# A graph layer with residual and norm on one core: both halves of a dense pair through TensorE in one go

## The chip, the cores and the metric

The kernel runs on one core of one Trainium2 chip. The metric is the device time of one execution in microseconds (us); smaller is better.

## The reference

The input is `x` (100000 nodes of 96 features, float32), 25000 edges `src -> dst` sorted by `dst`, and 32 edge features. Two convolutions with a leaky ReLU (slope 0.01) follow each other, then a residual and a norm over each row. `X` below is `x`, with all 100000 nodes in both convolutions; everything is float32.

```python
def _egnn_conv(x, src, dst, edge_attr, W_msg, W_edge, W_root, b):
    msg = x[src] @ W_msg + edge_attr @ W_edge
    agg = jax.ops.segment_max(msg, dst, num_segments=x.shape[0])
    agg = jnp.where(jnp.isneginf(agg), 0.0, agg)
    return agg + x @ W_root + b
c1 = leaky_relu(_egnn_conv(X, src, dst, edge_attr, W1_msg, W1_edge, W1_root, b1))
c2 = leaky_relu(_egnn_conv(c1, src, dst, edge_attr, W2_msg, W2_edge, W2_root, b2))
out = _layernorm(X + c2)
```

## The kernel before

A node without an incoming edge needs no aggregate: its output is `leaky(leaky(x @ W1_root + b1) @ W2_root + b2) + x`, normed. The kernel computes this for all 100000 nodes (the **dense** work), and apart from it, along the list of edges, the rows of the nodes that have incoming edges (the **edge** work), which it writes over the dense rows at the end.

**Dense work.** 98 pairs of 1024 nodes. A pair has two halves `h` of 512 nodes. Layer 1 is one matmul per half into half `h` of `ps_1` (`layer1`, L448, 96x512). ScalarE writes 0.01 times it into `c1t` (`dense_t1`, L579), VectorE takes the larger of the two (`dense_c1`, L774). Layer 2 is four matmuls per half (`layer2`, L458, 128x96 each, `c1t` as the weights) into half `h` of `ps_z`. Then ScalarE writes 0.99 times the positive part to `yo` (`dense_r`, L588), VectorE adds 0.01 times the sum and `x` (`dense_u`, L766) and both (`dense_y`, L781), takes the statistics (L792), and the two engines norm the eight rows of 96 (L605 and L802). SyncE loads `xtb` and `xn` two pairs ahead and stores `yo` (`load_pair`, `store_pair`). `ps_1` and `ps_z` exist once, with two halves each; `c1t` exists twice.

**Step d** of the dense work puts layer 2 of pair d-1 and layer 1 of pair d side by side. Each engine has its own fixed order within a step: TensorE `layer2(d-1, h)`, `layer1(d, h)` for one half, then for the other; ScalarE std(d-2), r(d-1, 0), t1(d, 0), then r(d-1, 1), t1(d, 1), norm(d-2); VectorE reciprocal and shift of d-2, u(d-1, 0), c1(d, 0), y(d-1, 0), then u, c1, y of half 1, then statistics of d-1 and its part of the norm of d-2.

**Edge work.** 49 chunks of 512 edges. Stage A (first layer): GpSimd gathers `x[src]` (four indirect DMAs per chunk, L261, a ring `g_src` of six chunks), TensorE turns them (`forward`, L434), multiplies (`product`, L438) and turns the running maxima back (L472); VectorE scans (L739). Then GpSimd scatters the maxima to a table (L283), which ScalarE's DMAs clear ahead of it. Stage B (second layer): GpSimd gathers from the table (L261), and rows of `x` by destination (L272, a ring `g_dst` of ten chunks); TensorE does `forward(g_src)`, `sums_back` of the chunk before (L505, L506, into `ps_n`), `forward(g_dst)`, a product (L438) and the root term (L542, L544); VectorE and ScalarE join these (L884, L844, L739, L904, L860; L571, L695, L657, L672). At the end GpSimd scatters the edge rows over the dense rows in `out` (L283), chunk by chunk, each chunk when the pairs below its last destination are stored (`s_stored`) and its own rows are done (`e_done`).

**How the dense steps are spread.** 14 steps run within stage A (one every 3 or 4 chunks), 35 while GpSimd scatters to the table (stage S, nothing else on TensorE), 25 within stage B (one every second chunk), and steps 75 to 98 after it, while GpSimd scatters to `out` (here: the tail). In A and B TensorE puts half 0 behind `forward(g_src)` and half 1 further down the chunk.

Of the kernel before, what the change touches and what calls it, by code (L numbers as in the profile page):

```python
# [5 lines left out]
N, D = 100000, 96  # L6
# [6 lines left out]
J = 8  # L13
HJ = J // 2
# [6 lines left out]
XR = 4  # L21
# [25 lines left out]
STEPS_A = spread(NA, NCH, 0)  # L47
STEPS_S = spread(NS, NCH, NA)
STEPS_B = spread(NM, NCH, NA + NS)
# [9 lines left out]
def gnn_kernel(nc, x, xt, src, dst, dst_next, dst_row, dst_prev, aside, eat,  # L59
# [18 lines left out]
    with ctx:  # L78
# [15 lines left out]
        wr1 = sb("wr1", [D + 1, D])  # L94
# [110 lines left out]
        d_1 = sem("d_1")  # L205
# [15 lines left out]
        def cols(j):  # L221
            return slice(j * P, (j + 1) * P)

        def row(j):
            return slice(j * D, (j + 1) * D)
# [4 lines left out]
        def half(h):  # L230
            return slice(h * CH, (h + 1) * CH)
# [90 lines left out]
        def _(sp):  # L322
# [12 lines left out]
            def load_pair(q):  # L335
                if not real(q):
                    return
                k = q % XR
                if q >= XR:
                    sp.wait_ge(d_1, 2 * (q - XR) + 2)  # L340
                sp.dma_start(xtb[0:D, k, :], xt[q]).then_inc(l_xt[k], 16)
                if q >= XR:
                    sp.wait_ge(d_y, 2 * (q - XR) + 2)
                if q < NQ - 1:
                    sp.dma_start(xn[:, k, :], x_q[q]).then_inc(l_xn[k], 16)
                else:
                    sp.dma_start(xn[0:TAIL, k, :], x_tail).then_inc(l_xn[k], 16)
# [76 lines left out]
        @block.tensor  # L424
        def _(pe):
            pe.wait_ge(s_ident, 1)
            pe.wait_ge(s_const, 9 * 16)
            pe.wait_ge(s_ones, 3)

            def forward(rows, done, landed=(), count=0):  # L430
                for r in range(TPC):
                    if landed:
                        pe.wait_ge(landed[r], count)
                    last = nc.tensor.transpose(ps_t[0:D, cols(r)], rows[:, row(r)], ident[:, :])  # L434
                last.then_inc(done, 1)

            def product(ps, w, t, done):
                nc.tensor.matmul(ps[0:D, :], w, t, start=True, stop=True).then_inc(done, 1)  # L438

            def layer1(q, h):  # L440
                if not real(q):
                    return
                k = q % XR
                if h == 0:
                    pe.wait_ge(l_xt[k], 16 * (q // XR) + 16)
                if q >= 1:
                    pe.wait_ge(d_c1, 2 * (q - 1) + h + 1)
                nc.tensor.matmul(ps_1[0:D, h, :], wr1[:, :], xtb[:, k, half(h)],  # L448
                                 start=True, stop=True).then_inc(d_1, 1)

            def layer2(q, h):
                if not real(q):
                    return
                pe.wait_ge(d_c1, 2 * q + h + 1)
                if q >= 1:
                    pe.wait_ge(d_y, 2 * (q - 1) + h + 1)
                for j in range(HJ):
                    last = nc.tensor.matmul(ps_z[:, h, row(j)], c1t[:, q % 2, cols(h * HJ + j)], wr2[:, :],  # L458
                                            start=True, stop=True)
                last.then_inc(d_2, 1)  # L460

            def dense(steps, h):
                for d in steps:
                    layer2(d - 1, h)
                    layer1(d, h)

            def maxima_back(c):
                pe.wait_ge(a_scan, c + 1)
                if c >= 1:
                    pe.wait_ge(a_nc, c)  # L470
                for r in range(TPC):
                    last = nc.tensor.transpose(ps_n[:, row(r)], mx1[:, c % 2, cols(r)], ident[0:D, 0:D])  # L472
                last.then_inc(a_n, 1)

            for t in range(NCH):
                k = t % R
                if t >= 1:
                    pe.wait_ge(a_xe, t)
                forward(g_src[:, t % RS, :], a_t, slot(l_src, t % RS), 16 * (t // RS) + 16)
                dense(STEPS_A[t], 0)  # L480
                if t >= 1:
                    maxima_back(t - 1)
                pe.wait_ge(l_ea[k], 16 * (t // R) + 16)
                if t >= 1:
                    pe.wait_ge(a_scan, t)
                pe.wait_ge(a_xe, t + 1)
                product(ps_m, wm1[:, :], xe[:, k, :], a_m)
                if t >= 1:
                    pe.wait_ge(a_rc, t)
                product(ps_r, wr1[0:D, :], xe[0:D, k, :], a_r)  # L490
                dense(STEPS_A[t], 1)
            maxima_back(NCH - 1)
            for t in range(NCH):
                for h in range(2):
                    dense(STEPS_S[t], h)

            def sums_back(c):
                pe.wait_ge(b_c1d, c + 1)
                pe.wait_ge(b_scan, c + 1)
                if c >= 1:  # L500
                    pe.wait_ge(e_y, c)
                else:
                    pe.wait_ge(a_nc, NCH)
                for r in range(TPC):
                    nc.tensor.matmul(ps_n[:, row(r)], c1d[:, c % 2, cols(r)], wr2[:, :], start=True, stop=False)  # L505
                    last = nc.tensor.matmul(ps_n[:, row(r)], mx2[:, c % 2, cols(r)], ident[0:D, 0:D],  # L506
                                            start=False, stop=True)
                last.then_inc(b_n, 1)

            for c in range(NCH + 1):  # L510
                e = NCH + c
                k = e % R
                if c < NCH:
                    if c >= 1:
                        pe.wait_ge(b_xd, c)
                    else:
                        pe.wait_ge(a_xe, NCH)
                    forward(g_src[:, e % RS, :], b_t, slot(l_src, e % RS), 16 * (e // RS) + 16)
                    dense(STEPS_B[c], 0)
                else:  # L520
                    dense(STEPS_B[c], 0)
                    dense(STEPS_B[c], 1)
                if c >= 1:
                    sums_back(c - 1)
                if c < NCH:
                    pe.wait_ge(l_dst[c % RD], 64 * (c // RD) + 64)
                    pe.wait_ge(b_z1, c + 1)
                    forward(g_dst[:, c % RD, :], b_own)
                    dense(STEPS_B[c], 1)
                    pe.wait_ge(b_c1, c + 1)  # L530
                    pe.wait_ge(l_ea[k], 16 * (e // R) + 16)
                    if c >= 1:
                        pe.wait_ge(b_scan, c)
                    else:
                        pe.wait_ge(a_scan, NCH)
                    product(ps_m, wm2[:, :], xe[:, k, :], b_m)
                    pe.wait_ge(b_xd, c + 1)
                    if c >= 1:
                        pe.wait_ge(b_c1d, c)
                    else:  # L540
                        pe.wait_ge(a_rc, NCH)
                    nc.tensor.matmul(ps_r[0:D, :], wr1[0:D, :], xd[:, c % 2, :], start=True, stop=False)  # L542
                    for r in range(TPC):
                        last = nc.tensor.matmul(ps_r[0:D, cols(r)], nat[:, c * TPC + r, :], ident[:, :],  # L544
                                                start=False, stop=r == TPC - 1)
                    last.then_inc(b_r, 1)
            for d in range(LATE + 1, NQ + 1):
                for h in range(2):
                    dense(range(d, d + 1), h)

        @block.scalar
        def _(act):
# [20 lines left out]
            def dense_t1(q, h):  # L573
                if not real(q):
                    return
                act.wait_ge(d_1, 2 * q + h + 1)
                if q >= 2:
                    act.wait_ge(d_2, 2 * (q - 2) + h + 1)
                nc.scalar.activation(c1t[0:D, q % 2, half(h)], ps_1[0:D, h, :],  # L579
                                     ACT.Copy, scale=SLOPE).then_inc(d_t1, 1)  # L580

            def dense_r(q, h):
                if not real(q):
                    return
                act.wait_ge(d_2, 2 * q + h + 1)
                if q >= YR and h == 0:
                    act.wait_ge(o_st[q % YR], 16 * (q // YR))
                nc.scalar.activation(yo[:, q % YR, halfrow(h)], ps_z[:, h, 0:HJ * D],  # L588
                                     ACT.Relu, scale=1.0 - SLOPE).then_inc(d_r, 1)
# [358 lines left out]
```

## Time and profile before

| | us |
|---|---|
| median of 3 runs (lowest, highest) | 1247.58 (1247.53, 1247.67) |
| the profiled execution's own time | 1245.89 |
| its span on the core | 1244.1 |

| engine | busy us | share of the span |
|---|---|---|
| TensorE | 1022.8 | 82% |
| GpSimd | 934.0 | 75% |
| VectorE | 822.3 | 66% |
| ScalarE | 691.9 | 56% |

The span is the stretch that the profiler saw on the core; the execution's own time has 1.8 us more around it. "Busy" counts instructions at work; GpSimd's time between two DMA issues is not in it. The mean granted clock of TensorE is 0.733 of its full speed.

### The profile page before, as it was taken

To read this page: it belongs to the slowest core of one execution; us is meant where nothing else is said; L and a number is where in the kernel's file an instruction comes from. 1 tells how busy PE (TensorE), PEld (TensorE's weight loads), DVE (VectorE), ACT (ScalarE), POOL (GpSimd) and SP (SyncE) were. 2 spreads that over 40 slices of the span, in tenths; PEclk is the share of its full clock that TensorE was granted. 3 is DMA by queue.
4 is the path that set the end of the run, shared out by engine and by line. 5 is a ranking of instruction groups with operands and counts; after the bars stand their busy time and mean duration, and the time that the engine had idled before them with its cause. 6 is when DMAs were issued, how large, how long until landed. Compare 5 with 4: busy or idle time off the path is not lost. (4 is left out here: it accounts for less than half of the span.)

```text
span 1244.1 us, 17633 instructions
## 1 busy us (share of the span) xinstructions
PE 1022.8 (82%) x4312; PEld 686.4 (55%) x4312; DVE 822.3 (66%) x1879; ACT 691.9 (56%) x1669; POOL 934.0 (75%) x986
## 2 busy tenths in 40 slices
PE   4777687789999999928888989889888899999920
PEld 2343343445666666516666666666666665666610
DVE  4454354557777777709777777777786787777730
ACT  2454354566666666606656566565565667666630
POOL 7777777777777777777777777777777777777775
PEclk9988788898555555559888888888897895555555
DMA  7877778789999777745564554655556446677520
GB/s 213 262 236 233 216 238 263 228 273 340 380 402 381 233 225 211 219 128 141 151 168 127 163 154 130 167 123 167 142 142 165 139 129 192 211 219 214 165 86 28
DMA packets 105950, 248.96 MB, mean 200 GB/s; under 512 B 26641, under 2 KB 27537, under 8 KB 105849
## 3 DMA queue, kind: packets, MB, share of 16 engines
q1 hardware_dynamic: 67432, 161.21, 42.4%
q0 software_dynamic: 31360, 48.23, 15.5%
q10 hardware_dynamic: 7056, 38.40, 8.1%
q8 instruction: 36, 0.59, 0.2%
q14 instruction: 66, 0.53, 0.1%
HBM read 141.94 MB, written 105.80 MB: 199 GB/s over the span
## 5 line engine op out<-in xcount | busy, mean ns | idle before, releaser
L458 PEld LDWEIGHTS ps_z<-wr,c1t 97*128 97x128 f32 x1568 | 305.0, 277 | 139.5 <-issue 117.2
L458 PE MATMUL ps_z<-wr,c1t 97*128 97x96 f32 x1568 | 301.0, 358 | 5.1 <-DVE yo L781 5.1
L448 PE MATMUL ps<-xtb,wr 97*96 97x512 f32 x392 | 304.0, 870 | 0.0
L605 ACT ACTIVATE yo<-yo,shift,rstd 128x96 f32<-128x96 f32 x638 | 238.1, 456 | 0.5 <-DVE shift L755 0.5
L283 POOL DMA_INDIRECT out<-nat,end_i x196 | 188.2, 960 | 59.8 <-issue 34.8
L283 POOL DMA_INDIRECT agg_table<-nat,end_i x196 | 188.0, 959 | 59.8 <-issue 48.2
L261 POOL DMA_INDIRECT g_src<-agg_table,src_i x196 | 186.2, 950 | 59.8 <-issue 55.8
L261 POOL DMA_INDIRECT g_src<-in_x,src_i x196 | 185.1, 944 | 61.0 <-issue 48.5
L272 POOL DMA_INDIRECT g_dst<-in_x,own_i x196 | 185.8, 948 | 59.7 <-issue 56.4
L774 DVE TENSOR_TENSOR c1t<-ps,c1t 96x512 f32<-96x512 f32 x196 | 134.3, 685 | 80.8 <-ACT c1t L579 80.3
L739 DVE TENSOR_TENSOR_SCAN mx<-mask,mx,ps_m 96x512 f32<-96x512 f32 x96 | 122.0, 1271 | 88.8 <-PE ps_m L438 88.7
L579 ACT ACTIVATE c1t<-ps 96x512 f32<-96x512 f32 x196 | 114.9, 586 | 88.3 <-PE ps L448 88.2
L438 PE MATMUL ps_m<-xe,wm 128*96 128x512 f32 x196 | 129.5, 748 | 31.8 <-ACT xe L571 25.2
L505 PE MATMUL ps_n<-wr,c1d 97*128 97x96 f32 x392 | 91.8, 322 | 57.7 <-DVE c1d L904 57.7
L766 DVE SCALAR_TENSOR_TENSOR ps_z<-ps_z,xn 128x384 f32<-128x384 f32 x196 | 110.6, 564 | 34.4 <-ACT yo L588 34.1
L434 PE MATMUL ps_t<-ident,g_src 128*96 128x128 f32 x392 | 71.4, 292 | 69.7 <-DMA g_src<-in_x,src_i 34.1
L588 ACT ACTIVATE yo<-ps_z 128x384 f32<-128x384 f32 x196 | 94.3, 481 | 59.7 <-PE ps_z L458 56.8
L505 PEld LDWEIGHTS ps_n<-wr,c1d 97*128 97x128 f32 x392 | 74.8, 231 | 77.3 <-DVE c1d L904 71.6
L792 DVE BATCH_NORM_STATS2 stat<-yo 128x6 f32<-128x192 f32 x392 | 112.7, 350 | 2.5
L434 PEld LDWEIGHTS ps_t<-ident,g_src 128*96 128x96 f32 x392 | 48.7, 133 | 114.5 <-issue 69.6
L781 DVE TENSOR_TENSOR yo<-ps_z,yo 128x384 f32<-128x384 f32 x196 | 106.6, 544 | 0.1
L506 PE MATMUL ps_n<-ident,mx 96*128 96x96 f32 x392 | 92.9, 327 | 0.0
(60 smaller groups left out, 1149.9 us busy)
## 6 DMA issues: line engine op xcount, KB each, us to landing
xtb<-in_xt SPq DMA_DIRECT2D x98, 384.0 KB, 5.7
xn<-in_x SPq DMA_DIRECT2D x97, 384.0 KB, 6.2
out<-yo SPq DMA_DIRECT2D x97, 384.0 KB, 5.8
agg_table<-zero ACTq DMA_DIRECT2D x48, 768.0 KB, 7.2
mask<-mask_row SPq DMA_DIRECT2D x98, 192.0 KB, 4.9
root_keep<-rt SPq DMA_DIRECT2D x49, 192.0 KB, 4.4
rt<-root_keep SPq DMA_DIRECT2D x49, 192.0 KB
xe<-in_eat SPq DMA_DIRECT2D x98, 64.0 KB, 3.4
```

The source lines that it names most:

```text
L261: nc.gpsimd.indirect_dma_start(out=g_src[:, e % RS, row(r)], out_offset=None, in_=rows, in_offset=bass.IndirectOffsetOnAxis(ap=src_i[:, t: ...
L272: nc.gpsimd.indirect_dma_start(out=g_dst[:, c % RD, row(r)], out_offset=None, in_=x, in_offset=bass.IndirectOffsetOnAxis(ap=own_i[:, t:t + ...
L283: nc.gpsimd.indirect_dma_start(out=rows, out_offset=bass.IndirectOffsetOnAxis(ap=end_i[:, t:t + 1], axis=0), in_=nat[:, t, :], in_offset=N ...
L434: last = nc.tensor.transpose(ps_t[0:D, cols(r)], rows[:, row(r)], ident[:, :])
L438: nc.tensor.matmul(ps[0:D, :], w, t, start=True, stop=True).then_inc(done, 1)
L448: nc.tensor.matmul(ps_1[0:D, h, :], wr1[:, :], xtb[:, k, half(h)], start=True, stop=True).then_inc(d_1, 1)
L458: last = nc.tensor.matmul(ps_z[:, h, row(j)], c1t[:, q % 2, cols(h * HJ + j)], wr2[:, :], start=True, stop=True)
L505: nc.tensor.matmul(ps_n[:, row(r)], c1d[:, c % 2, cols(r)], wr2[:, :], start=True, stop=False)
L579: nc.scalar.activation(c1t[0:D, q % 2, half(h)], ps_1[0:D, h, :], ACT.Copy, scale=SLOPE).then_inc(d_t1, 1)
L605: last = nc.scalar.activation(yo[:, q % YR, row(j)], yo[:, q % YR, row(j)], ACT.Identity, bias=shift[:, q % 2, j:j + 1], scale=rstd[:, q % ...
L739: V.tensor_tensor_scan(mx[:, c % 2, :], mask[:, mk, :], ps_m[0:D, :], first, ALU.min, ALU.max).then_inc(done, 1)
L774: V.tensor_tensor(t, ps_1[0:D, h, :], t, ALU.max).then_inc(d_c1, 1)
```

## The change

TensorE no longer works by halves. `layer1(q)` waits once, for both halves of `c1` of pair q-1, issues both 96x512 matmuls and raises `d_1` once, after the second. `layer2(q)` waits once, for both halves of `c1` and both halves of `y`, issues all eight matmuls and raises `d_2` once, after the eighth. Both halves stand where half 0 stood; the place of half 1 further down a chunk is gone. ScalarE, VectorE and SyncE keep their instructions and their order; the waits of ScalarE (`dense_t1`, `dense_r`) and of SyncE (`load_pair`) count pairs now, not halves. No instruction that computes is added or removed.

```diff
@@ -337,7 +337,7 @@
                     return
                 k = q % XR
                 if q >= XR:
-                    sp.wait_ge(d_1, 2 * (q - XR) + 2)
+                    sp.wait_ge(d_1, q - XR + 1)
                 sp.dma_start(xtb[0:D, k, :], xt[q]).then_inc(l_xt[k], 16)
                 if q >= XR:
                     sp.wait_ge(d_y, 2 * (q - XR) + 2)
@@ -437,32 +437,32 @@
             def product(ps, w, t, done):
                 nc.tensor.matmul(ps[0:D, :], w, t, start=True, stop=True).then_inc(done, 1)
 
-            def layer1(q, h):
+            def layer1(q):
                 if not real(q):
                     return
                 k = q % XR
-                if h == 0:
-                    pe.wait_ge(l_xt[k], 16 * (q // XR) + 16)
+                pe.wait_ge(l_xt[k], 16 * (q // XR) + 16)
                 if q >= 1:
-                    pe.wait_ge(d_c1, 2 * (q - 1) + h + 1)
-                nc.tensor.matmul(ps_1[0:D, h, :], wr1[:, :], xtb[:, k, half(h)],
-                                 start=True, stop=True).then_inc(d_1, 1)
-
-            def layer2(q, h):
-                if not real(q):
-                    return
-                pe.wait_ge(d_c1, 2 * q + h + 1)
+                    pe.wait_ge(d_c1, 2 * q)
+                for h in range(2):
+                    last = nc.tensor.matmul(ps_1[0:D, h, :], wr1[:, :], xtb[:, k, half(h)], start=True, stop=True)
+                last.then_inc(d_1, 1)
+
+            def layer2(q):
+                if not real(q):
+                    return
+                pe.wait_ge(d_c1, 2 * q + 2)
                 if q >= 1:
-                    pe.wait_ge(d_y, 2 * (q - 1) + h + 1)
-                for j in range(HJ):
-                    last = nc.tensor.matmul(ps_z[:, h, row(j)], c1t[:, q % 2, cols(h * HJ + j)], wr2[:, :],
+                    pe.wait_ge(d_y, 2 * q)
+                for j in range(J):
+                    last = nc.tensor.matmul(ps_z[:, j // HJ, row(j % HJ)], c1t[:, q % 2, cols(j)], wr2[:, :],
                                             start=True, stop=True)
                 last.then_inc(d_2, 1)
 
-            def dense(steps, h):
+            def dense(steps):
                 for d in steps:
-                    layer2(d - 1, h)
-                    layer1(d, h)
+                    layer2(d - 1)
+                    layer1(d)
 
             def maxima_back(c):
                 pe.wait_ge(a_scan, c + 1)
@@ -477,7 +477,7 @@
                 if t >= 1:
                     pe.wait_ge(a_xe, t)
                 forward(g_src[:, t % RS, :], a_t, slot(l_src, t % RS), 16 * (t // RS) + 16)
-                dense(STEPS_A[t], 0)
+                dense(STEPS_A[t])
                 if t >= 1:
                     maxima_back(t - 1)
                 pe.wait_ge(l_ea[k], 16 * (t // R) + 16)
@@ -488,11 +488,9 @@
                 if t >= 1:
                     pe.wait_ge(a_rc, t)
                 product(ps_r, wr1[0:D, :], xe[0:D, k, :], a_r)
-                dense(STEPS_A[t], 1)
             maxima_back(NCH - 1)
             for t in range(NCH):
-                for h in range(2):
-                    dense(STEPS_S[t], h)
+                dense(STEPS_S[t])
 
             def sums_back(c):
                 pe.wait_ge(b_c1d, c + 1)
@@ -516,17 +514,15 @@
                     else:
                         pe.wait_ge(a_xe, NCH)
                     forward(g_src[:, e % RS, :], b_t, slot(l_src, e % RS), 16 * (e // RS) + 16)
-                    dense(STEPS_B[c], 0)
+                    dense(STEPS_B[c])
                 else:
-                    dense(STEPS_B[c], 0)
-                    dense(STEPS_B[c], 1)
+                    dense(STEPS_B[c])
                 if c >= 1:
                     sums_back(c - 1)
                 if c < NCH:
                     pe.wait_ge(l_dst[c % RD], 64 * (c // RD) + 64)
                     pe.wait_ge(b_z1, c + 1)
                     forward(g_dst[:, c % RD, :], b_own)
-                    dense(STEPS_B[c], 1)
                     pe.wait_ge(b_c1, c + 1)
                     pe.wait_ge(l_ea[k], 16 * (e // R) + 16)
                     if c >= 1:
@@ -545,8 +541,7 @@
                                                 start=False, stop=r == TPC - 1)
                     last.then_inc(b_r, 1)
             for d in range(LATE + 1, NQ + 1):
-                for h in range(2):
-                    dense(range(d, d + 1), h)
+                dense(range(d, d + 1))
 
         @block.scalar
         def _(act):
@@ -573,16 +568,16 @@
             def dense_t1(q, h):
                 if not real(q):
                     return
-                act.wait_ge(d_1, 2 * q + h + 1)
+                act.wait_ge(d_1, q + 1)
                 if q >= 2:
-                    act.wait_ge(d_2, 2 * (q - 2) + h + 1)
+                    act.wait_ge(d_2, q - 1)
                 nc.scalar.activation(c1t[0:D, q % 2, half(h)], ps_1[0:D, h, :],
                                      ACT.Copy, scale=SLOPE).then_inc(d_t1, 1)
 
             def dense_r(q, h):
                 if not real(q):
                     return
-                act.wait_ge(d_2, 2 * q + h + 1)
+                act.wait_ge(d_2, q + 1)
                 if q >= YR and h == 0:
                     act.wait_ge(o_st[q % YR], 16 * (q // YR))
                 nc.scalar.activation(yo[:, q % YR, halfrow(h)], ps_z[:, h, 0:HJ * D],
```

TensorE in stage S, before (`ps_z` is layer 2, `ps` or `ps_1` layer 1; the semaphores that a row waits for stand in brackets):

```order
L458 MATMUL ps_z<-wr,c1t 128x96 [waits d_y,d_c1]
L458 MATMUL ps_z<-wr,c1t 128x96 x3
L448 MATMUL ps<-xtb,wr 96x512 [waits d_c1]
L458 MATMUL ps_z<-wr,c1t 128x96 [waits d_y,d_c1]
L458 MATMUL ps_z<-wr,c1t 128x96 x3
L448 MATMUL ps<-xtb,wr 96x512 [waits d_c1,l_xt3]
```

TensorE at the same place, now:

```order
L458 MATMUL ps_z<-wr,c1t 128x96 [waits d_y,d_c1]
L458 MATMUL ps_z<-wr,c1t 128x96 x7
L448 MATMUL ps<-xtb,wr 96x512 [waits d_c1,l_xt3]
L448 MATMUL ps<-xtb,wr 96x512
L458 MATMUL ps_z<-wr,c1t 128x96 [waits d_y,d_c1]
```

One group of eight and one of two take the place of two alternations of four and one, with one place to wait per step in place of two.

TensorE in a chunk of stage B that holds a dense step, before, from the end of `sums_back` to the next chunk:

```order
L506 MATMUL ps_n<-ident,mx 128x96
L434 MATMUL ps_t<-ident,g_dst 96x128 x4
L458 MATMUL ps_z<-wr,c1t 128x96 x4
L448 MATMUL ps<-xtb,wr 96x512
L438 MATMUL ps_m<-xe,wm 96x512
L542 MATMUL ps_r<-xd,wr 96x512
L544 MATMUL ps_r<-ident,nat 96x128 x4
L434 MATMUL ps_t<-ident,g_src 96x128 x4
```

The same chunk now, from its start (L503 and L504 are `sums_back`, four of each in turn):

```order
L434 MATMUL ps_t<-ident,g_src 96x128 x4
L458 MATMUL ps_z<-wr,c1t 128x96 x8
L448 MATMUL ps<-xtb,wr 96x512 x2
L503 MATMUL ps_n<-wr,c1d 128x96
L504 MATMUL ps_n<-ident,mx 128x96
L503 MATMUL ps_n<-wr,c1d 128x96
L504 MATMUL ps_n<-ident,mx 128x96
L503 MATMUL ps_n<-wr,c1d 128x96
L504 MATMUL ps_n<-ident,mx 128x96
L503 MATMUL ps_n<-wr,c1d 128x96
L504 MATMUL ps_n<-ident,mx 128x96
L434 MATMUL ps_t<-ident,g_dst 96x128 x4
```

The second half's five matmuls stood between `forward(g_dst)` and the product; they now stand ahead of `sums_back` and `forward(g_dst)`.

## Rows read from the trace of the kernel before

**Rows 1.** Windows: stage S, stage B, tail; busy per engine (x count), clock, DMA share, GB/s.

```profile
300.00:527.00 227.00, 225.10 (x667) 150.67 (x666) 175.47 (x473) 148.01 (x371) 172.11 (x181) 0.50 0.86 298
...
549.00:1010.00 461.00, 401.66 (x2192) 299.42 (x2193) 353.44 (x759) 273.59 (x676) 348.83 (x369) 0.86 0.55 145
1028.00:1190.00 162.00, 159.70 (x476) 107.20 (x476) 125.66 (x338) 109.82 (x279) 122.97 (x129) 0.50 0.64 196
```

**Rows 2.** Lines L261 and L283 on GpSimd: duration ns min/median/max, first and last start.

```profile
L261 POOL DMA_INDIRECT g_src<-in_x,src_i x196: 940/944/1115, 3.0 to 281.6; - x196
...
L283 POOL DMA_INDIRECT out<-nat,end_i x196: 954/958/1342, 987.1 to 1233.8; - x196
```

**Rows 3.** Timeline, TensorE's first work of stage B.

```profile
548.23 0.42 PE L434 MATMUL ps_t<-ident,g_src 128*96 128x128 f32 x1 [22.52 <-DMA g_src<-agg_table,src_i]
```

**Rows 4.** The page's DMA issues (to landing, us); the last store; GpSimd's last chunk.

```profile
out<-yo SPq DMA_DIRECT2D x97, 384.0 KB, 5.8
...
1195.36 0.34 SPq L358 DMA_DIRECT2D out<-yo  x1
...
1230.03 0.96 POOL L283 DMA_INDIRECT out<-nat,end_i  x1 [0.30 <-issue]
```

**Rows 5.** Timeline of stage S, one dense step.

```profile
421.34 1.86 PE L458 MATMUL ps_z<-wr,c1t 97*128 97x96 f32 x8
...
421.96 0.55 DVE L766 SCALAR_TENSOR_TENSOR ps_z<-ps_z,xn 128x384 f32<-128x384 f32 x1
...
422.43 0.68 DVE L774 TENSOR_TENSOR c1t<-ps,c1t 96x512 f32<-96x512 f32 x1
...
422.99 1.91 PE L448 MATMUL ps<-xtb,wr 97*96 97x512 f32 x2
...
424.70 1.86 PE L458 MATMUL ps_z<-wr,c1t 97*128 97x96 f32 x8
...
424.94 0.59 ACT L579 ACTIVATE c1t<-ps 96x512 f32<-96x512 f32 x1 [1.22 <-PE ps L448]
...
425.57 0.69 DVE L774 TENSOR_TENSOR c1t<-ps,c1t 96x512 f32<-96x512 f32 x1 [1.24 <-ACT c1t L579]
...
426.17 0.54 DVE L781 TENSOR_TENSOR yo<-ps_z,yo 128x384 f32<-128x384 f32 x1
```

**Rows 6.** Timeline of the tail: its first step and its last.

```profile
1027.79 1.99 PE L458 MATMUL ps_z<-wr,c1t 97*128 97x96 f32 x8 [1.50 <-DVE yo L781]
...
1029.58 1.92 PE L448 MATMUL ps<-xtb,wr 97*96 97x512 f32 x2
...
1186.32 0.54 DVE L781 TENSOR_TENSOR yo<-ps_z,yo 128x384 f32<-128x384 f32 x1
...
1187.01 1.99 PE L458 MATMUL ps_z<-wr,c1t 97*128 97x96 f32 x8 [0.31 <-DVE yo L781]
...
1189.40 0.56 DVE L781 TENSOR_TENSOR yo<-ps_z,yo 128x384 f32<-128x384 f32 x1
...
1189.87 0.56 DVE L766 SCALAR_TENSOR_TENSOR ps_z<-ps_z,xn 128x384 f32<-128x384 f32 x1
```

**Rows 7.** Timeline of stage B: a wait for c1d, and half 1 in the next chunk.

```profile
700.13 0.67 ACT L695 ACTIVATE c1d<-ps_r,b1s 96x512 f32<-96x512 f32 x1
...
701.64 0.46 PE L505 MATMUL ps_n<-wr,c1d 97*128 97x96 f32 x2 [2.53 <-DVE c1d L904]
...
714.23 1.03 PE L458 MATMUL ps_z<-wr,c1t 97*128 97x96 f32 x8
...
715.96 1.02 PE L438 MATMUL ps_m<-xe,wm 128*96 128x512 f32 x2
```

**Rows 8.** Windows, TensorE alone: length, busy (x count), clock, DMA share, GB/s.

```profile
702.60:705.90 3.30, 3.30 (x15) 0.50 0.84 249
```

**Rows 9.** Timeline of stage B: `forward(g_src)` of chunks 7 and 47.

```profile
611.63 0.60 PE L434 MATMUL ps_t<-ident,g_src 128*96 128x128 f32 x4
...
1001.29 0.60 PE L434 MATMUL ps_t<-ident,g_src 128*96 128x128 f32 x4
```

## The prediction, made before the changed kernel ran

> **What bounds the kernel now.** I read the windows by stage first. In stage S and in the tail TensorE is busy all the time (225.1 of 227.0 us, 159.7 of 162.0) at a granted clock of 0.50, that is 1.2 GHz; in stage B it has 0.86 on the mean, a mix of the two levels [rows 1]. That looks like a kernel bound by TensorE. The lines of GpSimd say otherwise: it issues its 980 indirect DMAs from 3.0 us to 1233.8 us [rows 2], one every 1230.8 / 979 = 1.257 us, from the first to the last without a hole, and the last of them end the kernel. So GpSimd's issues are the bound, and TensorE has slack in two places:
> - at the end of stage S it stands 22.52 us for the first gathered row of the table [rows 3];
> - at the end the last pair's store is issued at 1195.36 and takes some 5.8 us to land, at 1201.2; GpSimd starts the last chunk's scatter, the only one that needs it, at 1230.03 [rows 4]. That is 28.9 us.
>
> The change cannot make the kernel faster by more than GpSimd's own pace lets it, which it doesn't touch. The question is how much later TensorE gets, and whether that is more than the slack.
>
> **A dense step in stage S and the tail.** Before, a half takes 1.65 us of layer 2 and 1.71 us of layer 1 (421.34 to 422.99 to 424.70), a step 2 x 3.36 = 6.72 us, because ScalarE and VectorE work on one half while TensorE works on the other [rows 5]. Now TensorE goes through layer 2 and layer 1 of both halves and then has nothing: the next layer 2 waits for c1 and y of both halves. I follow one step from the start of layer 2:
> - layer 2: 1.79 us for the first four matmuls when the engine had stood (1027.79 to 1029.58) [rows 6], 1.65 for the other four: 3.44.
> - layer 1: 1.71 for the first half, then 1.95 from the start of the second to ScalarE's t1 (422.99 to 424.94) [rows 5]: 3.66. t1 of half 0 now waits for the second half too, since `d_1` is raised once.
> - VectorE in its order: c1(0) 0.63 after t1 begins (424.94 to 425.57), y(0) 0.60 later (425.57 to 426.17) [rows 5], u(1) 0.47 later (1189.40 to 1189.87) [rows 6], c1(1) 0.47 later (421.96 to 422.43) [rows 5], y(1) again 0.60.
> - from y(1) to TensorE's next layer 2: 0.69 (1186.32 to 1187.01) [rows 6].
>
> ScalarE keeps up: r(1) and t1(1) follow t1(0) and are done before VectorE needs them. The statistics, the norm, r(0) and u(0) lie beside TensorE's 7.1 us. The sum is 3.44 + 3.66 + 0.63 + 0.60 + 0.47 + 0.47 + 0.60 + 0.69 = **10.56 us a step instead of 6.72, 3.84 more**. TensorE stands some 3.5 us in each.
>
> That sum is at the lower clock. At full clock the two matmul parts halve, and the step is about 7.1 us. Which one holds? In stage B the clock falls to 0.50 right after TensorE stood 2.53 us (until 701.64) [rows 7, 8], and through all of stage S and the tail it stays at 0.50 with TensorE busy without a pause [rows 1]. With a pause of 3.5 us in every step and less work between, nothing in these rows speaks for a higher clock. I take 0.50 throughout, less 3.4 us for a first step that may still run at full clock.
>
> **Stage S:** 35 steps x 3.84 = 134.4, less 3.4, is 131.0; of this 22.5 is slack. Stage B starts **108.5 us** later. ScalarE's clears of the table come between its steps; the zones up to 25 are cleared in stage A and the rest by step 25 of the ticks, ahead of the scatters that need them, so GpSimd's scatters don't wait.
>
> **Stage A:** the second half's 3.4 us move ahead of the products, but a chunk waits for its gathered rows anyway, and only every third or fourth has a step. Nothing, if the 5.03 us per chunk of GpSimd stay the pace; without that cover 14 x 1.73 = 24 us at most.
>
> **Stage B.** A chunk with a step had the five matmuls of half 1 behind `forward(g_dst)`: 1.73 us (714.23 to 715.96) [rows 7]. They move ahead of `sums_back`. TensorE's own work in the chunk is the same, but ScalarE's edge relu, the copy of xd and the edge norm start 1.73 us later, and behind them in its order stand r(1), t1(1), the norm of eight rows and only then the c1d of the edge, for which TensorE waits in the next chunk (c1d at 700.13 and `sums_back` at 701.64, after 2.53 us of standing) [rows 7]. So that wait grows by all of 1.73. Two chunks take (1001.29 - 611.63) / 20 = 19.48 us [rows 9], now 21.21. GpSimd needs 16 issues x 1.257 = 20.1 for them, so TensorE sets the pace, and since a gather may be only six chunks ahead of it (the rings), GpSimd is held. From chunk 7 to 48 that is 20.5 x 1.73 = 35.5. The first seven chunks took 63.4 (548.23 to 611.63) [rows 3, 9]; 3.5 x 21.21 = 74.2 is 10.8 more. Together **+46 us**. Bounds: nothing, if the wait had a cover that I miss; and if the longer standing also costs the full clock for 2 us more in each of the 24, +70.
>
> **Tail.** From the layer 2 of its first step to that of its last 1187.01 - 1027.79 = 159.2 us [rows 6]; now 23 x 10.56 = 242.9: **+83.7**. The last pair's layer 2 ends 1.65 later before ScalarE may begin: **+1.7**.
>
> **The sum.** 108.5 + 46.3 + 83.7 + 1.7 = 240.2 us later, less 28.9 of slack: +211.3. GpSimd by itself would be earlier: it may scatter to `out` from about chunk 42 of stage B, 548 + 108 + 42 x 10.6 = 1101, and its 196 issues take 247 us, to 1348; the last chunks then wait for the stores of the tail. The profiled execution's 1245.89 becomes 1457.2. The median of the runs is 1.7 above the profiled one, so I say 1459.
>
> **Rivals.**
> - *The long run of layer 1 gives the full clock back for part of the steps.* In stage B the clock is at 0.50 from 702.6 to 705.9 in `sums_back` and the product [rows 8] and the mean of 0.86 [rows 1] needs it back at full soon after, each time. What TensorE did just before is a run of 512-column matmuls, and the change makes such a run, 3.4 us of layer 1, where two of 1.7 stood. If half of the steps had full clock, each of them saves 3.4: 29 x 3.4 = 100 us, 1359. Against it: the clock would rise near the end of that run, and the pause of 3.5 us follows at once. The Trainium skill (TensorE: Matmul & The Clock Gate, section "What's actually happening") has the lower clock as the default that sustained activity releases and idling brings back. By it alone stage S before should have run at full clock; rows 1 show 0.50 at 99% busy, so on that side the trace disagrees, while the fall after standing agrees. Chance 0.10.
> - *No slower at all: the full clock holds through the dense-only stages.* The sum is then 35 x (7.1 - 6.72) = 13 us in stage S, under the 22.5 of slack; 23 x 7.1 - 159.2 = 4 in the tail, and stage B at full clock is below GpSimd's 20.1. All is inside the 28.9: 1247.6. It decides for this case if a step takes under about 7.4 us in stage S. For it: the stages at 99% busy are at 0.50 and stage B, at 87%, has 0.86 [rows 1]; a step of 7.1 us has TensorE busy half the time. Against it: the fall after 2.53 us of standing [rows 7, 8]. Chance 0.07.
> - *Stage B stays at the lower clock too*, because the standing there grows from 2.5 to 4.2 us. The busy share and clock of rows 1 make TensorE's work at full clock 401.7 x 0.86 = 345 us; at half clock 690, plus 24 x 4.2 of standing, 791 in place of 74 + 20.5 x 21.21 = 509: 1741. Against it: the products that stand before each rise are untouched. Chance 0.03.
>
> **Numbers.** The forecast has 0.80. The range takes in its bounds, 24 us more for stage B and part of stage A's 24 above, 46 without stage B's cost below, and reaches down over the first rival: 1355 to 1500. What is left out is the other two rivals. About 0.2% (2.5 us) is what can be told from no change. Slower holds the forecast and two rivals, 0.92; same 0.07; faster 0.01.
>
> **What would show it.** In the profile after: stage S and the tail with TensorE busy about 65% and clock 0.50, one wait of some 3.5 us for `yo` (y) per step, layer 2 every 10.6 us; the first `forward` of stage B near 657 without its wait for the gather; GpSimd standing at L261 or L272 in stage B for TensorE and VectorE, and at L283 for SyncE's stores near the end. Steps of 7 us with clock 1.00 would show the second rival; an unchanged GpSimd without holes would make the forecast wrong.

## The result, and the profile after

| | before | changed |
|---|---|---|
| median, us | 1247.62 (1247.53 to 1248.57, 4 runs) | 1482.74 (1480.14 to 1486.41, 4 runs) |
| span of the profiled execution, us | 1244.1 | 1484.5 |

The ratio is 1.1887, 95% interval 1.1872 to 1.1901: 235 us slower. 1459 was forecast, with 1355 to 1500 as the range.

The windows of the changed kernel, for stage S, stage B and the tail (columns as in rows 1), answer to rows 1:

```profile
302.00:663.00 361.00, 242.13 (x682) 149.09 (x683) 175.74 (x479) 150.62 (x379) 207.82 (x217) 0.51 0.60 195
670.00:1183.00 513.00, 416.42 (x2192) 311.00 (x2191) 360.50 (x767) 273.05 (x681) 361.43 (x375) 0.82 0.50 135
1223.00:1456.00 233.00, 156.28 (x441) 96.04 (x441) 112.69 (x307) 97.69 (x246) 105.49 (x110) 0.51 0.40 126
```

TensorE is busy 242 of 361 us in stage S, 67% in place of 99%, and its clock is still at 0.51. The engine now has pauses, and it has the lower clock as well as before. In stage B the clock is 0.82 (before 0.86).

One step of stage S in the changed kernel, from its timeline, answers to rows 5:

```profile
422.36 3.62 PE L448 MATMUL ps<-xtb,wr 97*96 97x512 f32 x4
...
426.01 0.59 ACT L574 ACTIVATE c1t<-ps 96x512 f32<-96x512 f32 x1 [2.92 <-PE ps L448]
...
426.64 0.69 DVE L769 TENSOR_TENSOR c1t<-ps,c1t 96x512 f32<-96x512 f32 x1 [2.95 <-ACT c1t L574]
...
427.25 0.54 DVE L776 TENSOR_TENSOR yo<-ps_z,yo 128x384 f32<-128x384 f32 x1
...
427.71 0.55 DVE L761 SCALAR_TENSOR_TENSOR ps_z<-ps_z,xn 128x384 f32<-128x384 f32 x1
...
428.18 0.68 DVE L769 TENSOR_TENSOR c1t<-ps,c1t 96x512 f32<-96x512 f32 x1
...
428.78 0.54 DVE L776 TENSOR_TENSOR yo<-ps_z,yo 128x384 f32<-128x384 f32 x1
...
429.47 2.85 PE L458 MATMUL ps_z<-wr,c1t 97*128 97x96 f32 x12 [3.49 <-DVE yo L776]
```

This is the chain that the prediction added up. Layer 1 begins at 422.36, t1 of half 0 only at 426.01, after both halves; then c1(0), y(0), u(1), c1(1), y(1) on VectorE, one behind the other, and layer 2 of the next step at 429.47, after 3.49 us of standing. VectorE itself stood 2.95 us for t1 just before: the two engines wait for each other in turn. From the page:

```profile
L458 PE MATMUL ps_z<-wr,c1t 97*128 97x96 f32 x1568 | 298.3, 370 | 210.4 <-DVE yo L776 210.4
```

Before, the same line stood 5.1 us for `yo` (y), now 210.4.

GpSimd's waits in the changed kernel (us in total, times, longest):

```profile
POOL g_src L261 <- issue: 108.3, 355, 0.4
POOL out L283 <- POOLq L315: 105.8, 8, 27.1
POOL g_src L261 <- PE ps_t L434: 103.4, 16, 95.0
...
POOL g_dst L272 <- DVE ps_n L855: 40.9, 28, 13.0
```

Rows 2 had it issuing without a hole. Now it waits long in three places: 95.0 us once in stage B's ring, for TensorE's first `forward`; 13.0 and then many short waits for VectorE to free `g_dst`; and 105.8 in eight waits ahead of the scatters to `out` (L315 stands right behind GpSimd's wait for `s_stored`, the count of stored pairs). The first `forward` of stage B, which answers to rows 3, has lost its wait for the gathered row altogether:

```profile
669.54 1.06 PE L434 MATMUL ps_t<-ident,g_src 128*96 128x128 f32 x4
```

Where the 240.4 us between the two spans lie, from the start times of TensorE's rows in the two timelines:

| stretch | before, us | after, us | difference | forecast |
|---|---|---|---|---|
| start to stage S's first layer 2 | 292.09 | 302.29 | +10.2 | 0 |
| stage S to its last matmul's end | 233.6 | 367.2 | +133.6 | +131.0 |
| standing until stage B's first `forward` | 22.5 | 0 | -22.5 | -22.5 |
| `forward` of chunk 0 to that of chunk 48 | 461.8 | 513.4 | +51.6 | +46.3 |
| from there to the tail's first layer 2 | 17.8 | 26.9 | +9.1 | 0 |
| tail, first layer 2 to the last | 159.2 | 246.1 | +86.9 | +83.7 |
| last layer 2 to the end | 57.1 | 28.5 | -28.6 | -27.2 |

### The profile page after: what moved, and what is told of

It reads as the page before. It is cut to its first block and busy times, and to the rows that moved or that the text cites. A ratio compares the mean times of both kernels' runs of the same rounds, so it can differ in the third digit from the quotient of the medians.

```text
span 1484.5 us, 17536 instructions
## 1 busy us (share of the span) xinstructions
PE 1075.3 (72%) x4312; PEld 701.5 (47%) x4312; DVE 822.7 (55%) x1879; ACT 687.3 (46%) x1669; POOL 939.7 (63%) x986
## 5 line engine op out<-in xcount | busy, mean ns | idle before, releaser
L458 PE MATMUL ps_z<-wr,c1t 97*128 97x96 f32 x1568 | 298.3, 370 | 210.4 <-DVE yo L776 210.4
L458 PEld LDWEIGHTS ps_z<-wr,c1t 97*128 97x128 f32 x1568 | 283.3, 279 | 302.2 <-DVE c1t L769 302.2
L448 PE MATMUL ps<-xtb,wr 97*96 97x512 f32 x392 | 292.2, 889 | 0.0
L261 POOL DMA_INDIRECT g_src<-agg_table,src_i x196 | 191.5, 977 | 158.3 <-PE ps_t L434 99.4
L283 POOL DMA_INDIRECT out<-nat,end_i x196 | 188.4, 961 | 163.1 <-POOLq L315 105.8
L283 POOL DMA_INDIRECT agg_table<-nat,end_i x196 | 188.2, 960 | 59.7 <-issue 46.3
L261 POOL DMA_INDIRECT g_src<-in_x,src_i x196 | 185.4, 946 | 61.0 <-issue 50.6
L503 PE MATMUL ps_n<-wr,c1d 97*128 97x96 f32 x392 | 100.3, 348 | 91.5 <-DVE c1d L899 91.5
L503 PEld LDWEIGHTS ps_n<-wr,c1d 97*128 97x128 f32 x392 | 82.9, 255 | 111.1 <-DVE c1d L899 97.7
L448 PEld LDWEIGHTS ps<-xtb,wr 97*96 97x96 f32 x392 | 83.1, 238 | 89.9 <-issue 89.9
L504 PE MATMUL ps_n<-ident,mx 96*128 96x96 f32 x392 | 98.6, 344 | 0.0
```

Source lines behind the costliest of these rows:

```text
L261: nc.gpsimd.indirect_dma_start(out=g_src[:, e % RS, row(r)], out_offset=None, in_=rows, in_offset=bass.IndirectOffsetOnAxis(ap=src_i[:, t: ...
L283: nc.gpsimd.indirect_dma_start(out=rows, out_offset=bass.IndirectOffsetOnAxis(ap=end_i[:, t:t + 1], axis=0), in_=nat[:, t, :], in_offset=N ...
L448: last = nc.tensor.matmul(ps_1[0:D, h, :], wr1[:, :], xtb[:, k, half(h)], start=True, stop=True)
L458: last = nc.tensor.matmul(ps_z[:, j // HJ, row(j % HJ)], c1t[:, q % 2, cols(j)], wr2[:, :], start=True, stop=True)
```

## The experiments

In the kernels of the first four runs a function `whole(d)` says in which steps the halves go together. TensorE raises the semaphores by half in all of them; what differs is whether ScalarE and TensorE wait by half or for both. A ScalarE that waits for both halves' counts is held just as by a semaphore that is raised once. Their line numbers are three to six higher than before's.

### Signals by half (e1)

```diff
-                act.wait_ge(d_1, q + 1)
+                act.wait_ge(d_1, 2 * q + h + 1)
...
-                act.wait_ge(d_2, q + 1)
+                act.wait_ge(d_2, 2 * q + h + 1)
```

(TensorE raises `d_1` and `d_2` behind each half; its own waits stay one per layer and pair.)

> The changed kernel's order and its one wait per layer and pair stay, but TensorE raises d_1 and d_2 after each half, and ScalarE's t1 and r wait for their own half. Theory (the serial chain behind layer 1 is what costs): t1(0), c1(0), y(0) and u(1) now lie beside the second half of layer 1, and the step at the lower clock is 3.44 + 1.71 + 1.95 + 0.63 + 0.60 + 0.69 = 9.02 us, not 10.60; the pause of TensorE falls from 3.5 to some 1.9 us. Time about 1393 us. Rival A (the single increments are the whole cost): a step of about 6.8 us and a time near 1290. Rival B (the single waits are the whole cost, signals don't matter): step 10.6, time 1483.

Measured: 1388.59 us, ratio 1.1146 (1.1114 to 1.1179). The step is 9.07 us where 9.02 was expected, and the time 1388.6 where 1393 was. The last of the chain in this kernel's stage S:

```profile
431.52 0.59 ACT L585 ACTIVATE c1t<-ps 96x512 f32<-96x512 f32 x1 [0.73 <-PE ps L451]
...
432.15 0.69 DVE L780 TENSOR_TENSOR c1t<-ps,c1t 96x512 f32<-96x512 f32 x1
...
432.75 0.54 DVE L787 TENSOR_TENSOR yo<-ps_z,yo 128x384 f32<-128x384 f32 x1
...
433.44 2.85 PE L462 MATMUL ps_z<-wr,c1t 97*128 97x96 f32 x12 [1.96 <-DVE yo L787]
```

t1(1), c1(1), y(1), layer 2, nothing else behind layer 1 any more, and the pause is 1.96 us in place of 3.49. Raising the semaphores once is 94 of the 237 us; it is neither all of it nor nothing.

### Signals and waits by half, the order alone (e2)

```diff
-                pe.wait_ge(d_c1, 2 * q + 2)
+                pe.wait_ge(d_c1, 2 * q + h + 1)
                 if q >= 1:
-                    pe.wait_ge(d_y, 2 * q)
+                    pe.wait_ge(d_y, 2 * (q - 1) + h + 1)
```

(The same in `layer1`; layer 2 of both halves still comes before layer 1 of both.)

> As the run before, and TensorE's waits are by half too; what is left of the change is the order alone: layer 2 of both halves, then layer 1 of both, in the place of half 0. Theory: layer 2 of half 0 may start once y(0) is there, 0.45 us after the end of layer 1, so the step is 6.72 + 0.45 + 0.14 = 7.3 us; stage S then costs 20 us, inside its slack but for the 10 us that stage A ended later; stage B still about 50 us more, 9 between stage B and the tail, the tail 14 more, less 29 of slack: about 1298 us. Rival A (the order by itself stalls the other engines, whatever the waits): step 9 or more, time near 1390. Rival B (only the dense-only stages matter): under 1260.

Measured: 1286.52 us, ratio 1.0327 (1.0297 to 1.0357), a step of 7.37 us. TensorE in stage S:

```profile
426.54 3.70 PE L462 MATMUL ps_z<-wr,c1t 97*128 97x96 f32 x16 [0.25 <-DVE yo L787]
430.04 2.77 PE L451 MATMUL ps<-xtb,wr 97*96 97x512 f32 x3
```

The pause is down to 0.25 us. So in the dense-only stages little of the cost is the order of the matmuls (0.65 us a step, 7.37 for 6.72); most of it is that all of a pair is waited for and announced at once. From this run to the changed kernel a step grows by 1.70 us through the joined waits and by 1.53 through the joined signals. The time is 12 us under the 1298 expected. Some 6 of them lie ahead of stage B: stage S's first layer 2 comes at 296.79 us in this run, at 302.29 in the changed kernel. Where the rest lies was not traced.

### In stage S and the tail only (e3), in stages A and B only (e4)

```diff
+        def whole(d):
+            return NA <= d < NA + NS or d > LATE
```

(e3; e4 has `not (...)`.)

> Both halves in one go (with one wait on either side) only in stage S and the tail; stages A and B as in the kernel before. Theory: stage S 134 us longer less 22.5 of slack, tail 84 + 3 longer, less 28.9 of slack at the end: 1246 + 170 = 1416 us, steps of 10.6, and stage B takes the 462 us of the kernel before. Rival (the cost sits mostly where edge work is held up in stage B): under 1330.

> The counterpart: both halves in one go only within stages A and B, in the place of half 0; stage S and the tail as before, steps of 6.72. Theory: stage A ends 10 us later, which the 22.5 us before stage B hide; stage B 52 us longer, 9 more until the tail, less 28.9 of slack: 1246 + 32 = 1278 us. With the run before the parts make the whole: 170 + 32, and 29 of slack and 10 of stage A that both runs hide, are 241, against 240 measured. Rival (the stages' costs are not independent, a late stage S changes stage B): the sum misses 240 by over 15.

Measured: 1420.92 us, ratio 1.1406 (1.1373 to 1.1439), and 1269.91 us, ratio 1.0194 (1.0164 to 1.0223). In e3 the steps are 10.6 us, stage B starts at 660.59 and takes 463.7 us from `forward` of chunk 0 to that of chunk 48 (461.8 before). In e4 the steps of stage S and the tail stay at 6.72; the same stretch of stage B takes 511.0 us, so its whole cost is there. TensorE's last layer 2 starts 54.9 us later than before (1241.91 for 1187.01) and the span is only 23.9 longer: the slack at the end hides more than half.

The parts add up like this: 175.1 for e3 and 24.0 for e4; the 28.9 of slack at the end, which each of the two runs uses and the whole can use only once; and the 7.0 by which stage S starts later in e4 (299.06 for 292.09), which e4 hides in the slack ahead of stage B. That is 235, against 237 for the whole. To within 2 us the stages' costs are independent; what is shared is the slack, which can be used once.

### Sixteen scatters fewer, before and after (e7, e8)

```diff
-            for c in range(NCH):
+            for c in range(4, NCH):
                 last = (c + 1) * TPC - 1
```

(The counts of the waits behind it are lowered to match. Both kernels leave out the edge rows of the first four chunks; those rows of `out` stay the dense ones.)

> The kernel before without the scatters of the first four chunks into the output (16 of GpSimd's 980 indirect DMAs are left out, so these rows stay the dense ones). Theory (GpSimd's issues are the bound, TensorE has 28.9 us of slack at the end): 16 x 1.257 = 20.1 us less, 1245.9 to about 1225.8 us. Rival (TensorE, busy 82%, is the bound): no change.

> The changed kernel without the same 16 scatters. Theory (the bound has moved to TensorE's chain; GpSimd stands 100 us for the stores of the tail): no change, within 4 us of 1483. Rival (GpSimd's issues still add up with the rest): 20 us less, 1463.

Measured: 1224.96 us against 1246.03 for the kernel before, 21.1 less (ratio 0.9832, 0.9813 to 0.9851), and 1482.31 us for the changed one, no change against its 1482.74. This is the test of what bounds: before, 16 issues fewer on GpSimd save 21.1 us (16 x 1.257 is 20.1), though TensorE is busy for 82% of the time; after, the same 16 are worth nothing. In e8 the time freed is stood through at the end (126.2 us in place of 105.8):

```profile
POOL out L284 <- POOLq L316: 126.2, 8, 27.1
```

### The edge's c1d ahead of the dense norm on ScalarE (e9)

```diff
-                dense_tail(steps)
+                for d in steps:
+                    dense_r(d - 1, 1)
+                    dense_t1(d, 1)
                 if c < NCH:
                     ...
                     nc.scalar.activation(c1d[0:D, c % 2, :], ps_r[0:D, :], ACT.Identity,
                                          bias=b1s[:, :], scale=SLOPE).then_inc(b_t1, 1)
+                for d in steps:
+                    dense_norm(d - 2)
```

> The changed kernel, with ScalarE in a chunk of stage B doing the edge's c1d before the norm of the dense pair, not after. Theory (in stage B TensorE waits for c1d, which stands behind eight norm rows on ScalarE): two chunks take 21.65 - 2.97 = 18.7 us while GpSimd is still ahead, so stage B is some 60 us shorter: about 1420 us, and TensorE's waits for c1d fall under 1.5 us. Rival (the wait for c1d only covers another one, the scan or the gathers): under 20 us gained.

Measured: 1456.23 us, ratio 1.1687 (1.1659 to 1.1716): 26.5 us less than the changed kernel, under half of what was expected and more than the rival's 20. TensorE's wait for c1d, in the changed kernel and, below, in this one:

```profile
819.49 0.74 PE L503 MATMUL ps_n<-wr,c1d 97*128 97x96 f32 x2 [4.09 <-DVE c1d L899]
```

```profile
808.14 0.68 ACT L692 ACTIVATE c1d<-ps_r,b1s 96x512 f32<-96x512 f32 x1
808.28 0.69 DVE L773 TENSOR_TENSOR c1t<-ps,c1t 96x512 f32<-96x512 f32 x1
...
808.88 0.54 DVE L780 TENSOR_TENSOR yo<-ps_z,yo 128x384 f32<-128x384 f32 x1
...
809.35 1.27 DVE L738 TENSOR_TENSOR_SCAN mx<-mask,mx,ps_m 96x512 f32<-96x512 f32 x1
...
810.54 0.72 DVE L903 SCALAR_TENSOR_TENSOR c1d<-ps_r,b1c,c1d 96x512 f32<-96x512 f32 x1
...
811.31 0.73 PE L503 MATMUL ps_n<-wr,c1d 97*128 97x96 f32 x2 [2.89 <-DVE c1d L903]
```

ScalarE's part of c1d is done at 808.8, but VectorE has c1(1), y(1) and the scan ahead of its own part, and those stand behind r(1) and t1(1), which the change delays as well. The wait falls from 4.09 to 2.89 us, and no further. Two chunks take 20.46 us in place of 21.65; 24 x 1.19 = 29 us is about what was gained. The norm on ScalarE was only the last of two things in the way. With it gone, c1d waits for VectorE's own order, and that comes only 1.2 us earlier.

### The order of the change, by half, with c1d ahead (e12)

The edits of e2 and e9 together.

> The order of the change, with signals and waits by half (e2_waits_by_half), and ScalarE's c1d ahead of the dense norm in stage B (e9_c1d_ahead). Theory (the parts are independent): stage B 26 us shorter than in e2_waits_by_half as it was in e9_c1d_ahead against the changed kernel, of which all counts since the tail sets the end: 1286.5 - 26 = 1260 us. Rival (the norm now held up delays the stores or the next step): 1275 or more.

Measured: 1258.64 us, against 1249.64 us for the kernel before on that chip: ratio 1.0067 (1.0044 to 1.0090); 1260 was expected. The gains of the two nearly add up: e2 is 40.7 us above its kernel before and e9 takes 26.5 off the changed kernel, which leaves 14, and 9.0 is measured. With all waits and signals by half and c1d moved ahead, what is left of the change costs 0.7%. It doesn't beat the kernel before; with GpSimd's issues as the bound (e7) no other result of moving TensorE's work was to be expected.

### Two and four more matmuls in the pause (e10, e11)

```diff
                     layer1(d)
+                    if NA <= d < NA + NS or d > LATE:
+                        for i in range(2):
+                            nc.tensor.matmul(ps_m[0:D, :], wr1[0:D, :], mx1[:, 0, :], start=True, stop=True)
```

(e11 has `range(4)`. Nothing reads the results.)

> The changed kernel with two more 96x512 matmuls, into ps_m, which nothing reads then, behind layer 1 of each step of stage S and the tail (about as long, 3.4 us at the lower clock, as TensorE's pause). Theory A (the pause is what keeps the clock down; with 512-column matmuls in it the full clock comes back and holds, the chain of the step stays): a step of 7.1 us with the clock at 1.00, stage B starts only some 3 us late, in all 1290 us. Theory B (the clock stays at 0.50 with TensorE busy, as in stage S of the kernel before): the step stays at 10.6 or grows a little, 1483 to 1495 us.

> As e10_two_extra, with four more matmuls behind layer 1 in each step of stage S and the tail in place of two. With two, steps took 7.2 us where the clock was full and about 10 where it was not, in turns, and at full clock the pause was still 1.8 us. Theory A (with no pause left at full clock the clock holds): nearly all steps 7.2 us, TensorE's clock at 1.00 in stage S, about 1290 us. Theory B (extra work only lengthens the step where the clock is low): steps of 13.9 us at 0.50, the time well above 1483, up to 1670. If the clock still goes back and forth, between the two.

Measured: 1405.88 us (1399.24 and 1412.52; ratio 1.1283, 1.1193 to 1.1374), and 1294.07 us (ratio 1.0355, 1.0323 to 1.0387). TensorE in stage S with two, with the pause in brackets:

```profile
400.81 3.70 PE L458 MATMUL ps_z<-wr,c1t 97*128 97x96 f32 x16 [1.72 <-DVE yo L779]
404.30 3.62 PE L448 MATMUL ps<-xtb,wr 97*96 97x512 f32 x4
407.72 3.49 PE L468 MATMUL ps_m<-mx,wr 96*96 96x512 f32 x4
411.41 2.00 PE L458 MATMUL ps_z<-wr,c1t 97*128 97x96 f32 x16 [0.20 <-DVE yo L779]
413.24 1.88 PE L448 MATMUL ps<-xtb,wr 97*96 97x512 f32 x4
414.96 1.88 PE L468 MATMUL ps_m<-mx,wr 96*96 96x512 f32 x4
418.61 2.00 PE L458 MATMUL ps_z<-wr,c1t 97*128 97x96 f32 x16 [1.77 <-DVE yo L779]
```

Neither theory held: the same eight matmuls take 3.70 us, then 2.00. The granted clock goes from 1.2 to 2.4 GHz and back, and the steps are 7.2 us in some cases and 10 to 10.6 in others. With four, the window of stage S (columns as in rows 1):

```profile
302.00:545.00 243.00, 241.31 (x932) 122.77 (x932) 170.71 (x464) 146.12 (x366) 184.51 (x193) 0.99 0.82 278
```

The mean clock is 0.99, and every step behind the first takes 7.2 us; 1290 was expected for the time. The clock was not simply kept from stage A. The stage begins at the lower one, and the full one comes back within the first extra matmuls:

```profile
298.50 3.70 PE L458 MATMUL ps_z<-wr,c1t 97*128 97x96 f32 x16 [1.36 <-DVE yo L779]
301.99 3.62 PE L448 MATMUL ps<-xtb,wr 97*96 97x512 f32 x4
305.41 4.84 PE L468 MATMUL ps_m<-mx,wr 96*96 96x512 f32 x8
310.08 1.92 PE L458 MATMUL ps_z<-wr,c1t 97*128 97x96 f32 x16
```

236 matmuls that compute nothing of use take 189 us off the changed kernel. The order of the work and the waits in a step are those of the changed kernel; the extra matmuls fill TensorE's pause, and the clock is another. The steps at full clock take 7.20 us in e10 too, with 1.77 us of pause left in them, so 7.20 is the length of the chain and not that of TensorE's work. The changed step is thus 10.60 us at the lower clock and 7.20 at the full one; against the 6.72 of the kernel before at its lower clock that is 3.88 more in the one case and 0.48 in the other. The kernel before did not pay for its lower clock in its time, since GpSimd's issues set that (e7) and TensorE's steps had slack.

## Why the prediction was right, and where it was off

The mechanism is the one foretold, and the range held the time. Point by point:

- **GpSimd's issues bound the kernel before.** Shown by e7 and e8.
- **The step of stage S and the tail.** 10.56 us was added up, 10.60 measured, and each link of the chain lies in the timeline where the prediction put it. e1 (9.07 for 9.02) and e2 (7.37 for 7.3) take the chain apart link by link.
- **The clock stays at 0.50.** Measured 0.51 in both stages. The two rivals that had more clock, for half of the steps or for all, didn't come. The step that the second of them gave, 7.1 us, is right for that clock: e11 has 7.2. The Trainium skill (TensorE: Matmul & The Clock Gate, section "What's actually happening") has sustained activity release the lower clock. In e11 the trace agrees; in stage S before, with TensorE just as busy (225.1 of 227.0 us, rows 1), it does not.
- **Stage B.** The place of the growth was right: the wait for c1d went from 2.53 us [rows 7] to 4.09, and e4 has stage B's 50 us alone. Two chunks take 21.65 us where 21.21 was expected [rows 9], 2.17 more than before. That is not the wait alone. These are TensorE's waits (us in total, times, longest), then its busy time and clock, from `forward` of chunk 7 to that of chunk 47, before and changed (windows with columns as in rows 1):

```profile
PE ps_n L505 <- DVE c1d L904: 50.5, 20, 2.5
PE ps_n L503 <- DVE c1d L899: 81.8, 20, 4.1
611.63:1001.29 389.66, 339.15 (x1842) 254.13 (x1841) 298.47 (x640) 234.09 (x580) 294.87 (x312) 0.85 0.56 147
741.22:1174.17 432.95, 351.12 (x1843) 263.43 (x1841) 301.94 (x640) 232.19 (x580) 310.97 (x322) 0.81 0.50 134
```

The wait grew by 1.57 us per two chunks, where the prediction had 1.73. The same matmuls take 0.60 us more per two chunks at a lower mean clock, where the prediction took nothing and had 2 us as its bound. Of the norm on ScalarE the prediction said that c1d stands behind it; e9 shows that taking it away shortens the wait by 1.20 us only, and that VectorE's scan behind y(1) is next.

- **The rival in which stage B stays at the lower clock** didn't come: 0.82.

The median came out 24 us above the forecast. The profiled executions that the table compares differ by 29 more than the sum of 211.3; the profiled one is the slowest of the four and 3.7 us above their median, and the forecast had taken the median as 1.7 above the profile. By terms the 29 lie as follows.

The step that failed most is "Stage A: nothing", with the reason that a chunk waits for its gathered rows anyway. Stage S starts 10.2 us later in this trace (the `forward` of the last chunk at 293.24 for 285.82, then a wait for y). GpSimd did keep its pace: it issued the stage's last gather at 281.9 us, before at 281.6. The waits of TensorE over the first 285 us (us in total, times, longest), before and then changed, show that the cover was there, but that other waits grew beside it:

```profile
PE ps_t L434 <- DMA g_src<-in_x,src_i: 34.1, 28, 4.2
PE ps_m L438 <- ACT xe L571: 25.2, 29, 2.6
...
PE ps_m L438 <- ACT xe L566: 33.0, 25, 3.6
PE ps_t L434 <- DMA g_src<-in_x,src_i: 17.1, 15, 4.2
...
PE ps_n L472 <- DVE mx L734: 5.5, 10, 0.6
```

The waits for gathered rows gave up 17.0 us, those for ScalarE's `xe` grew by 7.8, and 5.5 for the running maxima are new. The bound of 24 was in the range; the value taken was the lower end.

Second is a term that the sum didn't have: between `forward` of chunk 48 and the tail lie two more dense steps among the last edge work, and that stretch grew by 9.1 us. Then come 5.3 us in stage B, which are the lower clock named above, less what the first chunks and the wait came out under their terms, and 3.2 in the tail: some 0.9 for a step that is 0.04 longer, the rest the tail's first step, which takes 13.0 us (1209.83 to 1222.80) and not 10.6. Stage S is off by 2.6 only because two errors nearly cancel, which is luck: 3.4 us were taken off for a first step at full clock, but it ran at the lower one (3.70 us for layer 2, from 302.29); and the last step was given its pause, though `forward` follows it at once, which saves 3.5.

Not settled: how much of the 10 us of stage A comes from a lower clock (0.82 in place of 0.88 from 200 to 285 us) and how much from the later products. The other runs with whole pairs in stage A have that `forward` at 289.5 to 292.4. No run changed stage A alone.

## What to carry to other kernels

Two halves that travel by themselves through a chain of engines are a pipeline. Waiting once for both and announcing once for both turns it into nearly one engine at a time, and no row here shows anything saved by it. The engine whose busy share is highest need not be the bound: look for the one that issues without a hole, and count each slack once. And where a stage runs at the lower clock without costing time, a change that puts TensorE's matmuls into the chain begins to pay for that clock. Price the step at both levels and find out which one the new pattern will have.

## What the runs showed of the hardware that was not expected

TensorE busy for 99% of a stage ran at 1.2 GHz in the kernel before (0.50, rows 1), and busy for 99% of a stage ran at 2.4 GHz in e11 (0.99). The grouping of a pair's matmuls does not make the difference: e2 has the order of e11 without the extra matmuls, and TensorE is busy there for 96% of stage S at 0.52:

```profile
310.00:530.00 220.00, 211.26 (x607) 129.37 (x608) 157.62 (x423) 133.20 (x335) 166.95 (x175) 0.52 0.83 281
```

What differs in e11 is the four more 96x512 matmuls per step. Why they bring the full clock is not shown; what these rows do show is that the busy time in the profile does not tell which of the levels will be granted. With two such matmuls per step the level went up and down all through the stage (mean 0.75 in stage S), and two executions of that kernel differ by 13 us, more than those of any other kernel here; next are the four of the changed kernel, with 6 us.
